# A routed mixture-of-experts kernel: order of its first DMAs, of two tables' work and of its last sums

## The reference

```python
y = _rmsnorm(x, norm_w);  y_conv = conv3(y) + conv_b;  y_ssm = scan(h = tanh(a) * h + b * y)
x = x + y_conv + y_ssm;   z = _rmsnorm(x, mlp_norm_w)
x = x + (silu(z @ w_gate + b_gate) * (z @ w_up + b_up)) @ w_down + b_down
x = layernorm(x_in + x)
scores = sigmoid(x @ gate_w.T)        # T x 64, choice: scores + gate_bias
gmask  = best 4 of 8 groups of 8 experts, by the sum of a group's two best
topk   = best 8 experts inside those groups; weights = scores / their sum * 2.5
out    = sum over topk of weight * (silu(x @ Wg.T) * (x @ Wu.T)) @ Wd.T   # hidden 88 per expert
       + the same form with the shared weights Sg, Su, Sd (hidden 176)
x = layernorm(x + out)
```

## Time and profile before

| | us |
|---|---|
| median of 3 runs (lowest, highest) | 713.38 (713.14, 715.68) |
| the profiled execution | 719.66 |
| its span, first to last instruction | 717.9 |

### The profile page before, as it was taken

The page is one execution under the profiler, slowest core; times in us unless marked ns, Lnnn a source line. Parts: engine busy times, 40 slices in busy tenths (PEclk is TensorE's granted clock), DMA queues, the critical chain, the costliest instruction groups (busy, mean ns, idle before and its releaser), DMA issues.

```text
span 717.9 us, 13379 instructions
## 1 busy us (share of the span) xinstructions
PE 598.1 (83%) x3456; PEld 479.0 (67%) x3457; DVE 456.1 (64%) x1300; ACT 319.5 (45%) x626; POOL 448.4 (62%) x464
## 2 busy tenths in 40 slices
PE   3976899788895998999977989999968999999400
PEld 2745666355554998999967989999825566666200
DVE  3564788878364686767763675637412899869524
ACT  8555667645450453555533445555411234252201
POOL 1005257777777777777757777777610477777772
PEclk9997999989997998999987999999989999999855
DMA  8999611111113676777755878888631123222211
GB/s 217 214 243 343 157 49 51 49 50 50 54 54 98 199 226 182 222 225 223 207 145 163 227 223 226 226 232 226 191 99 41 34 51 95 52 66 66 66 51 52
DMA packets 124397, 101.32 MB, mean 141 GB/s; under 512 B 15126, under 2 KB 114286, under 8 KB 123886
## 3 DMA queue, kind: packets, MB, share of 16 engines
q1 hardware_dynamic: 63558, 48.41, 24.9%
q0 software_dynamic: 14336, 29.39, 14.4%
q10 hardware_dynamic: 46464, 23.07, 11.2%
HBM read 52.58 MB, written 48.23 MB: 140 GB/s over the span
## 4 chain that ended last, share of the span: by engine, by line
POOL 37%; PE 25%; issue 16%; DMA 11%; DVE 6%; ACT 3%; SPq 1%; POOLq 0%; DVEq 0%; ACTq 0%
POOL xs_dram L482 30%; PE GU L786 7%; POOL arena L487 7%; DMA xs_dram<-x1r,slots 5%; PE OT L806 5%; DMA arena<-os_dram,gslots 4%; PE XT L775 3%; PE HT L795 3%; DVE x_all L1521 2%; DVE key L1558 1%; DMA os_dram<-ol 1%; PE GU L717 1%; PE GU L567 1%; PE GU L718 1%; PE OT L588 1%
## 5 line engine op out<-in xcount | busy, mean ns | idle before, releaser
L482 POOL DMA_INDIRECT xs_dram<-x1r,slots x224 | 228.6, 1020 | 140.8 <-issue 64.4
L487 POOL DMA_INDIRECT arena<-os_dram,gslots x224 | 217.7, 972 | 115.7 <-issue 62.0
L786 PE MATMUL GU<-wgu_sb,arena 128*128 x704 | 124.5, 321 | 0.0
L786 PEld LDWEIGHTS GU<-wgu_sb,arena 128*128 128x128 f32 x704 | 109.7, 197 | 0.3 <-issue 0.2
L1467 DVE TENSOR_TENSOR mlpw_sb<-GU,mlpw_sb 128x352 f32<-128x352 f32 x88 | 46.1, 524 | 99.4 <-ACT mlpw_sb L1048 78.5
L806 PE MATMUL OT<-wd_sb,arena 88*128 x704 | 96.3, 281 | 2.1 <-ACT ol L1058 1.7
L1058 ACT ACTIVATE ol<-OT 128x512 f32<-128x512 f32 x88 | 52.5, 597 | 91.0 <-PE OT L806 91.0
L806 PEld LDWEIGHTS OT<-wd_sb,arena 88*128 88x128 f32 x704 | 87.3, 195 | 4.4 <-issue 3.4
L1521 DVE SCALAR_TENSOR_TENSOR x_all<-arena,wk,x_all 128x128 f32<-128x128 f32 x224 | 64.2, 345 | 29.5 <-DMA arena<-os_dram,gslots 28.4
L775 PE MATMUL XT<-ident,arena 128*128 128x128 f32 x352 | 56.4, 285 | 14.0 <-DMA arena<-xs_dram 9.6
L1048 ACT ACTIVATE mlpw_sb<-GU 128x352 f32<-128x352 f32 x88 | 40.8, 463 | 51.4 <-PE GU L786 50.4
(11 more groups left out here) (195 smaller groups left out, 887.3 us busy)
## 6 DMA issues: line engine op xcount, KB each, us to landing
arena<-xs_dram SPq DMA_DIRECT2D x352, 64.0 KB
os_dram<-ol ACTq DMA_DIRECT2D x88, 256.0 KB
xs_dram<-ol SPq DMA_DIRECT2D x4, 2048.0 KB, 26.1
...
xs_dram<-x1r,slots POOLq DMA_INDIRECT x224
arena<-os_dram,gslots POOLq DMA_INDIRECT x224, 2.6
...
```

Source lines behind the costliest of these rows:

```text
L482: g.indirect_dma_start(out=xs[b], out_offset=bass.IndirectOffsetOnAxis(ap=slots[:, t * K + k:t * K + k + 1], axis=0), in_=x1r[:, t, :], in ...
L487: return g.indirect_dma_start(out=gbuf[:, g_ % 2, t - SETS[g_][0], k, :], out_offset=None, in_=os[batch_of(t)], in_offset=bass.IndirectOff ...
L786: ins = mm(GU[:, 2 * r + i // 2, (i % 2) * 2 * I:(i % 2 + 1) * 2 * I], xg[:, r, i * P:(i + 1) * P], wgu_sb[:, bass.ds(at[i], 2 * I)], star ...
```

## The change

Four things change.

- SP sends the two expert weights ahead of the fills. The fills are cut into sixteen DMAs of 512 KB (eight for each batch's buffer), and SP issues piece i when scatter 4i has landed.
- `gather_slots(1)` is done in two halves of 7 tiles, behind quads 12 and 14 of batch 0, instead of whole behind quad 11. The first 16 quads of DVE's program are now written out, before the first 12.
- The sums of sets 2 and 3 move out of the dense experts: four rounds of set 2 stand behind the last four quads of batch 1, the other four and all of set 3 between the shared expert's chunks 4 to 7.
- Inside the dense experts the sums of sets 4 to 7, the statistics and the roots come at other blocks; a third root is taken inside the loop instead of behind it.

```diff
@@ -79,6 +79,8 @@
 HI = I // 2
 NJ = E * I // P
 LAG = 8
+FILL_PARTS = 8
+FILL_EVERY = 4
 assert all(n * P + P <= STRIDE for n in TILES) and all(n % QUAD == 0 for n in ET) and P == 2 * E and NJ == HI
 
 
@@ -103,9 +105,9 @@
 
 
 SUM_AT = {0: 60, 1: 76}
-SUMS_IN_DENSE = {2: (0, 1, 8), 3: (8, 2, 8), 4: (12, 2, 8), 5: (18, 1, 8), 6: (34, 1, 8)}
-STATS_IN_DENSE = {0: 0, 1: 1, 9: 2, 17: 3, 27: 4, 42: 5}
-ROOT_AT = (11, 29)
+SUMS_IN_DENSE = {4: (2, 2, 8), 5: (10, 1, 8), 6: (26, 1, 8), 7: (38, 1, 5)}
+STATS_IN_DENSE = {0: 0, 1: 1, 2: 2, 7: 3, 19: 4, 35: 5}
+ROOT_AT = (5, 21, 37)
 ROOTS = ((0, 3), (3, 5), (5, 6), (6, NC))
 
 
@@ -370,14 +372,14 @@
             def load_x(c):
                 sp.dma_start(x_all[:, span(c), :], x_t[:, span(c), :]).then_inc(d_x[c], 16)
 
-            def fill(b):
-
-                n = P // 2 // K
+            def fill(b, i):
+
+                n = P // K // FILL_PARTS
+                h = i % 2
                 pads = xs[b].rearrange("(e r) d -> e (r d)", r=STRIDE)
-                for h in range(2):
-                    sp.dma_start(pads[:, h * n * K * P:(h + 1) * n * K * P].rearrange("e (n c) -> e n c", n=n),
-                                 flat(ol[h * E:(h + 1) * E, 0:2, :]).unsqueeze(1).to_broadcast([E, n, K * P])
-                                 ).then_inc(d_fill[b], 16)
+                sp.dma_start(pads[:, i * n * K * P:(i + 1) * n * K * P].rearrange("e (n c) -> e n c", n=n),
+                             flat(ol[h * E:(h + 1) * E, 0:2, :]).unsqueeze(1).to_broadcast([E, n, K * P])
+                             ).then_inc(d_fill[b], 16)
 
             sp.dma_start(vec[:, :], vecs).then_inc(s_vec, 16)
             load_x(0)
@@ -392,11 +394,14 @@
             sp.dma_start(gbias_sb[:, :], gate_bias.partition_broadcast(P)).then_inc(s_shw, 16)
             sp.dma_start(sgu_sb[:, :, :, :], sgu).then_inc(s_shw, 16)
             sp.dma_start(sd_sb[:, :, :], sd).then_inc(s_shw, 16)
+            sp.dma_start(wgu_sb[:, :], wgu).then_inc(s_expw, 16)
+            sp.dma_start(wd_sb[:, :], wd).then_inc(s_expw, 16)
             sp.wait_ge(s_zero, 1)
             for b in range(NBAT):
-                fill(b)
-            sp.dma_start(wgu_sb[:, :], wgu).then_inc(s_expw, 16)
-            sp.dma_start(wd_sb[:, :], wd).then_inc(s_expw, 16)
+                for i in range(FILL_PARTS):
+                    n = (b * FILL_PARTS + i) * FILL_EVERY
+                    sp.wait_ge(d_scat[n % LAG], 16 * (n // LAG + 1))
+                    fill(b, i)
 
 
             def load(b, q, u, held):
@@ -416,7 +421,7 @@
             sp.wait_ge(s_x1r, NC)
             for b in range(NBAT):
                 sp.wait_ge(s_woff, b + 1)
-                sp.wait_ge(d_fill[b], 32)
+                sp.wait_ge(d_fill[b], 16 * FILL_PARTS)
                 for i in range(LAG):
                     sp.wait_ge(d_scat[i], 16 * K * TFIRST[b + 1] // LAG)
                 for u in range(0, UN, 2):
@@ -491,7 +496,7 @@
             for g_, ts in enumerate(SETS):
                 b = batch_of(ts[0])
                 if ts[0] == TFIRST[b]:
-                    pool.wait_ge(s_gslot, b + 1)
+                    pool.wait_ge(s_gslot, 2 * b + 1)
                     for r in range(4):
                         pool.wait_ge(d_st[r], 4 * Q0[b + 1])
                 for k in range(K):
@@ -1100,7 +1105,7 @@
             norm_v(NS)
             nc.scalar.preload_act_table(ACT.Silu)
             for b in range(NBAT):
-                act.wait_ge(d_fill[b], 32)
+                act.wait_ge(d_fill[b], 16 * FILL_PARTS)
             for c in range(SH_A):
                 for j in range(SJ):
                     shared_silu(c, j)
@@ -1352,9 +1357,8 @@
                 v.tensor_tensor(woff[0:1, 2, n], HT[0:1, H_OFF:H_OFF + ET[b]], trow[0:1, 0, 0:ET[b]],
                                 ALU.add).then_inc(s_woff, 1)
 
-            def gather_slots(b):
-
-                lo, hi = TFIRST[b], TFIRST[b + 1]
+            def gather_slots(b, lo, hi):
+
                 dve.wait_ge(s_ended, b + 1)
                 then(v.tensor_tensor(key[:, lo:hi, :], key[:, lo:hi, :], bc(delta[:, b, :].unsqueeze(1), P, hi - lo, E),
                                      ALU.add))
@@ -1454,7 +1458,7 @@
                     place_tiles(NBAT - 1)
             add_shared(SH_A - 1)
             weight_columns(NBAT - 1)
-            gather_slots(0)
+            gather_slots(0, 0, TFIRST[1])
 
             def is_at_least(q, n):
                 return not isinstance(q, int) or q >= n
@@ -1581,8 +1585,11 @@
                     add_round(g, k)
 
             mul_h(0, 0)
-            for q in range(3 * UN):
+            for q in range(4 * UN):
                 quad(0, q, q)
+                if q in (12, 14):
+                    lo = TFIRST[1] + (q - 12) // 2 * (TILES[1] // 2)
+                    gather_slots(1, lo, lo + TILES[1] // 2)
                 if q % 2:
                     slot_weights(q // 2, 3 * (q // 2))
                 if q == 2:
@@ -1595,8 +1602,7 @@
                     mask_groups()
                 if q == 10:
                     choose(NS)
-            gather_slots(1)
-            weighed(0, 3 * UN, Q0[1] - UN)
+            weighed(0, 4 * UN, Q0[1] - UN)
             for q in range(Q0[1] - UN, Q0[1]):
                 quad(0, q, q)
                 if q % 2:
@@ -1610,17 +1616,24 @@
             plain(1, SUM_AT[0] + K, SUM_AT[1])
             adding(1, 1)
             plain(1, SUM_AT[1] + K, NQ - UN)
-            for q in range(max(NQ - UN, SUM_AT[1] + K), NQ):
+            for q in range(NQ - UN, NQ):
                 quad(1, q, q)
+                add_round(2, q - (NQ - UN))
 
             for c in range(SH_A, NC):
                 shared_hidden(c, 0)
                 shared_hidden(c, 1)
                 if c > SH_A:
                     add_shared(c - 1)
+                if c < SH_A + 2:
+                    add_round(2, UN + 2 * (c - SH_A))
+                    add_round(2, UN + 2 * (c - SH_A) + 1)
+                else:
+                    for k in range(UN):
+                        add_round(3, UN * (c - SH_A - 2) + k)
             add_shared(NC - 1)
 
-            done_of = dict.fromkeys(range(2, NSET), 0)
+            done_of = dict.fromkeys(range(4, NSET), 0)
             for j in range(NJ):
                 dense_product(j)
                 for g, (first, each, most) in SUMS_IN_DENSE.items():
@@ -1636,8 +1649,7 @@
                     if j == at + 1:
                         inverse_deviation(r)
 
-            inverse_deviation(2)
-            for g in range(2, NSET):
+            for g in range(4, NSET):
                 for k in range(done_of[g], K - (g == NSET - 1)):
                     add_round(g, k)
             dve.wait_ge(p_dd, NJ)

```

## The result

| | before | changed |
|---|---|---|
| median of 4 runs each, us (lowest, highest) | 714.53 (713.14, 716.25) | 675.71 (671.72, 676.24) |
| the profiled execution, and its span | 719.66, 717.9 | 671.72, 670.0 |
| mean granted clock of PE | 0.931 | 0.964 |

The ratio of changed to before is 0.9447, 95% interval 0.9408 to 0.9486. The forecast was 661.7 us with 653 to 674: the direction and most of the size came, and the median lies 1.7 us above the range.

What follows compares the result with a forecast made beforehand. Bound by POOL's scatters stalled behind SP's queue, then set 4's gathers waiting for DVE's sums. Batch 1 19.1 us earlier, last gather 51.9 earlier, span 51.7 less: 668.0 profiled, 661.7 as the median, range 653 to 674.

Steps and rivals of the forecast that it cites:

- the scatters' stream: POOL's scatters: without the stall behind queued loads, the last starts at 352.1 instead of 371.22.
- batch 0's start: PE at batch 0: loads come before 221.9, saving 6.3 us of waiting, 8.8 us with the clock kept.
- the gather slots: DVE's slot block in batch 0: two halves stop holding up PE, 6.2 us gained, bounds 0 and 6.2.
- The moved sums: Sums of sets 2 and 3 hidden behind batch 1's last quads and between shared chunks; PE pays 1.0 us.
- the rival at 12.7 us: DVE's moved sums are not hidden and cost 12.7 us more, time 674; chance 0.05.
- The slower rival: Fill pieces stall POOL's scatters, 4.0 us each, time 824, chance 0.04; mild form 679, chance 0.03.
- The 2.4 us for a piece: SP's queue: each 512 KB fill piece takes 2.4 us of every 5.1 at 222 GB/s.
- 6.3 subtracted: Profiled execution (719.66) lay 6.3 us above the median (713.38), so 668.0 profiled becomes 661.7 as the median.
- the first gather of set 4: POOL: needs only batch 1's stores, so starts at 509.5 instead of 561.40, which followed a 38.07 us standstill.
- The term of 19.1 us for the scatters' stall: POOL's early scatters: no stall puts number 32 at 99.1 instead of 118.2; batch 1 starts 19.1 us earlier.
- if PE loses one of the terms above, it decides instead: Batch 1's start: scatters decide by less than 1 us over PE, unless PE loses one of its forecast gains.
- the rival in which PE keeps its losses: Slot halves still stall PE and its clock stays low at batch 0: batch 1 gains 10.7, time 670; chance 0.09.

Runs made afterwards that it cites:

- before2: The kernel before, unchanged, run once more for a second trace: 718.51 us.
- before_deep: The kernel before with four gather rounds in flight instead of two in two-tile sets: 716.42 us, ratio 1.0001.
- slots_only: The kernel before with only the gather slots of batch 1 in two halves: 713.94 us, ratio 0.9934.
- dma_only: The kernel before with only weights first and fills in sixteen pieces: 711.71 us, ratio 0.9886.
- ungated: The changed kernel with the fill pieces no longer waiting for scatters to land: 675.70 us, ratio 0.9419.
- weights_last: The changed kernel with the sixteen fill pieces sent without waits ahead of the weights: 674.57 us, ratio 0.9416.
- deep3: The changed kernel with eight gathers in flight instead of four in two-tile sets: 669.90 us, ratio 0.9345.
- late_wdf: The changed kernel with SP's two 1 MB dense weight loads moved behind its wait for the last stores: 673.43 us, ratio 0.9397.
- the pair on one chip: The changed kernel with eight instead of four gathers in flight in two-tile sets (671.75 us), beside the changed kernel itself (677.14 us).
- sums_only: The kernel before with only the moved sums, statistics and roots: 684.16 us, ratio 0.9498.
- no_dma: The changed kernel with fills and weights as in the kernel before: 682.87 us, ratio 0.953.
- again_pair: The changed kernel itself, run on the chip of a version with deeper gathers: 677.14 us, ratio 0.9442.
- again: The changed kernel itself, run once more for a second trace: 676.40 us, ratio 0.9407.
- no_slots: The changed kernel with the gather slots of batch 1 as one block behind quad 11: 676.30 us, ratio 0.9443.

## Why the prediction was wrong in size

Right, and within 1 us in the first trace: the scatters' stream (last at 351.74, forecast 352.1), batch 0's start, the gather slots (5.7 us gained where 6.2 were forecast), batch 1 (358.57 for 359.2), set 4 to the last sum, the end. The moved sums were hidden but for 1.9 us by the first traces ("shared" to the dense blocks 35.5 us, before 33.6), and but for 1.0, as forecast, by the averages of five traces of the changed kernel (35.5) and of five with the sums in their old place (34.5: before, before2, before_deep, slots_only, dma_only); so the rival at 12.7 us fell. The slower rival fell whole: with a piece in flight 4.5 us of about 5.1 no scatter waited. The 2.4 us for a piece was mis-sized, and it did no harm. No row shows how a scatter and the transfers beside it take turns, so why the fills of `ungated` let 17 scatters through in 56 to 80 us and the weights of `weights_last` only 12 stays open.

The median missed by 14.0 us. In numbers of the sum: 3.7 between the forecast for the profiled execution and what that took (668.0 and 671.72), and 10.3 in the step from it to the median (6.3 subtracted; the traced execution of the changed kernel lay 4.0 below its median).

**The 3.7: the first gather of set 4.** This step of the prediction failed. It said that these gathers need only the stores, 509.5. They also stand behind set 3 on POOL, and set 3, cut to four gathers in flight, met SP's loads. It started at 514.30, 4.8 late; 0.8 came back on the way to the last sum (145.1 for 145.9), and 0.3 that had been allowed for DVE's copy was not needed. `deep3`, `late_wdf` and the pair on one chip (5.4 us) show the cause, `before_deep` why nothing of it was visible. I had read the 38.07 us of the earlier trace rows as one wait; it covered a second, shorter one.

**The 10.3: two single executions taken as typical.** The term of 19.1 us for the scatters' stall was mis-sized. The sum took the whole 19.1 us of stall from one trace. Six executions with that program lose 12.6 to 19.3 us between scatters 0 and 15 beyond the 19.75 of an unstalled one (slots_only 13.4, before2 15.4, before_deep 16.2, sums_only 17.7, before 19.3; `no_dma`, with scatter 15 at 88.9, 12.6): the trace I forecast from was the worst. In the other direction, three of the five traces of the changed kernel have batch 0 beginning partly at half clock (0.71, 0.64 and 0.64 granted in 222 to 236 us), and batch 1 at 361.8 to 363.7. PE, within 1 us of the scatters by the sum, decides there: batch 1 starts 11.1 to 12.5 us behind the last scatter, where the other two traces have 6.8 and 6.9. The clause "if PE loses one of the terms above, it decides instead" was the usual case. From batch 0's start to batch 1's these three take 138.4 to 138.5 us, the other two 136.4 and 136.5. PE no longer loses time at the gather slots (5.7 us gained); of the rival in which PE keeps its losses, the half on the clock came true.

The table bears both out. "Shared" starts on average at 517.9 in the four executions before, before2, before_deep and sums_only, and at 503.6 in the five of the changed kernel: 14.4 us instead of 19.1, so 4.7 lost. From there to set 4's first gather the five take 13.5 us instead of the forecast's 509.5 - 501.1 = 8.4, so 5.1 lost, 4.5 of them in set 3. Together 9.8 of a forecast gain of 51.7. The measured gain is 38.8 against 714.53 here, and 40.5 (`again_pair`) and 42.1 (`again`) elsewhere. What remains is the base: 713.38, the median of three runs, is lower than each of the six medians of before measured since (714.53 to 718.53). What decides in which execution PE's clock falls stays open.

That the parts alone sum to 49 us and the whole to 42.6 has in part the same root. In `sums_only` and `no_dma` POOL stands idle between set 3 and set 4, waiting for the stores, so set 3's own waits cost nothing there; in the five traces of the whole they cost 3.1 to 5.9 us (set 4's first gather, less the end of ACT's wait and 0.83). Set 4's first gather in `sums_only`, then in `no_dma`:

```profile
527.72 0.94 POOL L487 DMA_INDIRECT arena<-os_dram,gslots  x1 [8.29 <-issue]
```

```profile
520.62 0.95 POOL L487 DMA_INDIRECT arena<-os_dram,gslots  x1 [12.11 <-issue]
```

The second part's 4.7 us alone are not explained, and `no_slots` shows it worth nothing measurable in the whole.
